# A four-layer graph network on one core: 23 single source blocks instead of 15, the maximum as one reduction, and a node stage spread over three engines

## The chip, the cores and the metric

The kernel runs on one core of one Trainium2 chip. The metric is the device time of one launch in microseconds (us). A launch holds everything: sorting out the graph, encoding nodes and edges, four layers, and the output. Lower is better.

## The reference

There are 6250 nodes with 64 features and 206,250 directed edges (100,000 pairs in both directions and one self loop per node), sorted by target node. `h` is the encoded node table, `e` the encoded edge table. Four layers of this run one after the other:

```
msg   = relu(h[src] + e) + 1e-7                # one row of 64 per edge
m     = msg * t                                # t: one number per layer
ex    = exp(m - segment_max(m, dst)[dst])      # softmax over a node's edges
agg   = segment_sum(msg * ex, dst) / segment_sum(ex, dst)
z     = relu(layernorm((h + agg) @ w1 + b1) * g1 + bb1)
h_new = z @ w2 + b2                            # added to h from the second layer on
```

Between layers `h` goes through a layer normalization, gain, bias and relu; behind the last one the input `x` is added.

## The kernel before

**Stage 1** (`prepare`) encodes edges and nodes and works out which edges belong to which node. **Stage 2** (`lay`) puts the 6250 nodes into 49 blocks of 128 (one node per partition) and gives each block `d` a row of `S[d]` slots of 64 features. The first `G` slots of a block are a grid: slot `s` holds the edge whose source lies in group `s` of source nodes, a group being one source block of 128 or a pair of them. Edges that find no free grid slot go to the `V[d]` overflow slots behind it. Before the change there are 15 single blocks and 17 pairs, so G = 32, and the 49 blocks have 676 overflow slots and 2244 slots in all. For 35 blocks (18 units) stage 2 forms the slot rows with matmuls: for each of the 128 nodes a one-hot matrix `hot` (DVE, L886) times the node's rows in `byk` (PE, L905, five nodes to a PSUM bank, 102 columns each of which 65 are used), copied out by ACT.

**Stage 3** is the four layers (`layer`), three in a loop and one behind it. Within a layer the blocks go by in a fixed order in which large and small rows of slots alternate. For block `d`:

- `gathers(d)`: POOL issues one indirect DMA for each overflow slot, from `ztab` into `gb` (L1228). `gb` has two buffers; the gathers of d+1 wait until `over(d-1)` has read its buffer.
- `load_x(d)`, `load_oh(d)`: SP's queue loads the encoded edges `xb` and the 49 one-hot matrices `oh` of a block (1568 KB), two buffers each. `load_oh(d+2)` waits for the products of block d.
- `passes(d, j)`: PE multiplies `oh` with the node table `zp`, 147 small matmuls (L1243) for a block, for the eight grid slots j of a PSUM bank each; `gps` is a ring of four banks.
- `add(d, j)`: DVE adds a bank of products to `xb` (L1260). `over(d)` adds the gathered rows (L1270).
- `most(d)`: the maximum over the slots, by halving (L1281, five or six operations) and a last one into `top_x` (L1286); ACT makes `cm` of it.
- `sub(d, i)`: per slice of up to 24 slots, relu and minus the maximum (DVE, L1302), then ACT's exp (L1308).
- `mul(d, i)`: relu times the exponential (DVE, L1316), then the slot sums: PE adds the slots with an identity matrix in `both` (L1326), two matmuls of 512 columns for every four slots. `fold(d)` brings them down to 128 columns (L1336).
- `node_unit(u)`: softmax division, linear 1, layer normalization, linear 2, update of `h`, normalization of the next table rows, split into three bf16 parts, scatter to `ztab`; for two blocks at a time. It is a generator that `steps` advances in pieces between the operations above.

All engines run their own instructions in the order in which the code writes them. One trip of the block loop is:

```python
for j in range(JS):
    add(d, j)
    if d + 1 < ND:
        passes(d + 1, j)
    steps(2, "normed")
over(d)
...                      # most(d), sub(d, i), fold(d - 1), node head
for i in range(n):
    mul(d, i)            # and its slot sums on PE
```

So PE's order is: slot sums of block d-1, all 147 products of block d+1, slot sums of block d. The normalization (`norm`) runs on DVE alone; its inverse root is an integer start value and three Newton steps on columns of two numbers (L201 to L220), and the normalized rows are made by L247.

## Time and profile before

| | |
|---|---|
| median of three runs | 6420.68 us (6414.47 to 6424.67) |
| the profiled execution | 6423.57 us, its span 6419.1 us |
| busy: PE, DVE, POOL, ACT | 72%, 75%, 69%, 27% of the span |
| stage 1, 2, 3 | 0 to about 840, to about 1792, to the end |
| a layer of the loop | about 1147 us; the last 1187 us |

A page gives the busy share of each engine over the span; what the time hangs on changes from stage to stage, and within a stage it is seen in the rows in order of time, by what an engine was idle for and until whom.

### The profile page before, as it was taken

The numbers are of one execution on the slowest core, as the hardware profiler recorded it, in microseconds if no ns is written. First come the engines' busy times: TensorE is split into PE (matmuls) and PEld (weight loads), VectorE is DVE, ScalarE is ACT, GpSimd is POOL, SyncE is SP. The second block draws the span as 40 slices with busy tenths as digits, with TensorE's granted clock in tenths as the row PEclk, the third lists the DMA queues.
The fourth block names the chain that finished last, engine by engine and source line by source line (L and its number), as shares of the span: only waits on it lengthen the run. The fifth ranks groups of instructions, "written<-read, shape, count | busy, mean of one in ns | idle before, by whom it ended". The sixth has DMA issues, their size and how long they took to land. (4 is left out here: it accounts for less than half of the span.)

```text
span 6419.1 us, 112465 instructions
## 1 busy us (share of the span) xinstructions
PE 4606.3 (72%) x44676; PEld 3217.7 (50%) x44676; DVE 4837.2 (75%) x10914; ACT 1753.4 (27%) x2619; POOL 4403.1 (69%) x3850
## 2 busy tenths in 40 slices
PE   6716888899947777773777777377777746767776
PEld 6705778888834444442444444244444433444443
DVE  9432555544359999994999999499999958888887
ACT  2403778666611111110111111011111101111111
POOL 2054767666357777875777777477777747777776
PEclk8956988776668888886888888688888878888887
DMA  8962565544365555544555554445555534444442
GB/s 346 417 205 81 211 224 197 214 179 164 124 202 164 168 178 171 169 130 128 169 170 174 166 170 159 115 156 176 170 171 171 168 124 141 162 158 165 158 158 85
DMA packets 313907, 1116.65 MB, mean 174 GB/s; under 512 B 138994, under 2 KB 142244, under 8 KB 252308
## 3 DMA queue, kind: packets, MB, share of 16 engines
q1 hardware_dynamic: 163444, 839.13, 35.3%
q0 software_dynamic: 134800, 214.63, 13.7%
q10 hardware_dynamic: 15120, 55.50, 2.1%
q8 instruction: 360, 5.90, 0.4%
q14 instruction: 183, 1.50, 0.1%
HBM read 859.44 MB, written 249.52 MB: 173 GB/s over the span
## 5 line engine op out<-in xcount | busy, mean ns | idle before, releaser
L1228 POOL DMA_INDIRECT gb<-ztab,ovi x2704 | 3158.9, 1168 | 971.2 <-issue 825.2
L1326 PE MATMUL bank<-ep_mid,keep 128*128 128x512 f32 (+3 forms) x3474 | 1610.3, 623 | 18.0 <-DVE ep_mid L1316 18.0
L1326 PEld LDWEIGHTS bank<-ep_mid,keep 128*128 128x128 f32 x3474 | 709.6, 207 | 884.3 <-issue 819.5
L1379 PE MATMUL bank<-keep,na 128*128 128x128 f32 x100 | 47.5, 475 | 1028.6 <-DVE na L1376 1028.6
L1292 ACT ACTIVATE cm<-top_x,nt 128x64 f32<-128x64 f32 x196 | 68.2, 348 | 2569.7 <-DVE top_x L1286 2569.7
L1065 POOL DMA_INDIRECT ecell<-zpw,ptg x588 | 611.2, 1040 | 226.9 <-issue 177.1
L1243 PE MATMUL bank<-zpw,oh_mid 128*128 128x64 bf16 x21609 | 660.4, 194 | 108.8 <-DMA oh_mid<-ohd 102.9
L1243 PEld LDWEIGHTS bank<-zpw,oh_mid 128*128 128x128 bf16 x21609 | 656.2, 98 | 150.2 <-issue 139.6
L905 PE MATMUL bank<-byk,zpw 88*88 88x102 f32 (+13 forms) x4608 | 639.3, 314 | 17.1 <-DVE zpw L886 13.2
L905 PEld LDWEIGHTS bank<-byk,zpw 88*88 88x88 f32 (+13 forms) x4608 | 607.9, 216 | 22.9 <-DVE zpw L886 15.7
L1260 DVE TENSOR_TENSOR xb<-bank,xb 128x512 f32<-128x512 f32 x784 | 535.6, 686 | 90.5 <-DMA xb<-ecell 90.2
L1326 PE MATMUL bank<-ep_last,keep 128*128 128x512 f32 (+3 forms) x1158 | 550.4, 636 | 2.9 <-DVE ep_last L1316 2.9
L1379 PEld LDWEIGHTS bank<-keep,na 128*128 128x128 f32 x100 | 18.2, 182 | 1040.8 <-DVE na L1376 1040.8
L886 DVE TENSOR_TENSOR zpw<-keep,kct 88x440 f32<-88x440 f32 (+13 forms) x468 | 291.8, 634 | 288.4 <-PE bank L905 284.2
L1308 ACT ACTIVATE ep_mid<-ep_mid,pack 128x1280 f32<-128x1280 f32 (+10 forms) x327 | 444.8, 1390 | 218.0 <-DVE ep_mid L1302 214.8
L1302 DVE SCALAR_TENSOR_TENSOR ep_mid<-xb,top_x 128x1280 f32<-128x1280 f32 (+10 forms) x327 | 489.2, 1540 | 14.9
L1316 DVE SCALAR_TENSOR_TENSOR ep_mid<-xb,ep_mid 128x1280 f32<-128x1280 f32 (+10 forms) x327 | 489.0, 1523 | 0.5 <-ACT ep_mid L1308 0.5
L1281 DVE TENSOR_TENSOR mx<-mx 128x128 f32<-128x128 f32 (+10 forms) x788 | 429.5, 545 | 20.0
L1270 DVE TENSOR_TENSOR xb<-gb,xb 128x768 f32<-128x768 f32 (+17 forms) x196 | 211.7, 1080 | 276.1 <-DMA gb<-ztab,ovi 275.3
L1326 PEld LDWEIGHTS bank<-ep_last,keep 128*128 128x128 f32 x1158 | 241.7, 212 | 300.2 <-issue 281.2
L1457 POOL DMA_INDIRECT ztab<-zb,wri x147 | 203.3, 1383 | 214.3 <-DVE zb L1448 172.5
L1281 DVE TENSOR_TENSOR mx<-xb 128x1408 f32<-128x1408 f32 (+10 forms) x196 | 332.7, 1697 | 3.1
(222 smaller groups left out, 6604.6 us busy)
## 6 DMA issues: line engine op xcount, KB each, us to landing
oh_mid<-ohd SPq DMA_DIRECT2D x147, 1568.0 KB
oh_last<-ohd SPq DMA_DIRECT2D x49, 1568.0 KB
ea_in<-in_ea SPq DMA_DIRECT2D x101, 512.0 KB, 8.2
enc<-es_out ACTq DMA_DIRECT2D x101, 512.0 KB, 8.8
gb<-ztab,ovi POOLq DMA_INDIRECT x2704
ohd<-oh_lay SPq DMA_DIRECT2D x49, 576.0 KB
xb<-ecell SPq DMA_DIRECT2D x20, 1408.0 KB
ohd<-oh_lay SPq DMA_DIRECT2D x49, 512.0 KB
```

What stands on the lines that cost most here:

```text
L886: k["hot"][g] = V(VE.tensor_tensor(hot[0:kp, g % 3, 0:n, 0:mp], iota1[0:kp, None, 0:mp].broadcast_to([kp, n, mp]), kct[0:kp, a:a + n][:, : ...
L905: q = PE.matmul(b[0:mp, WIDE * j:WIDE * j + WIDE], hot[0:kp, g % 3, j, 0:mp], byk[0:kp, at_d:at_d + WIDE], start=True, stop=True)
L1065: at["sc"][j, h] = sc_l[h](GP.indirect_dma_start(T["ecell"], bass.IndirectOffsetOnAxis(ap=ptg[:, j % 2, e:e + 1], axis=0), prows[:, h, a:a ...
L1228: at["g"][d] = ga_l[d % 2](GP.indirect_dma_start(gb[d % 2][:, 64 * v:64 * v + 64], None, T["ztab"], bass.IndirectOffsetOnAxis(ap=ovi[:, i: ...
L1243: q = PE.matmul(gps[j % n_gp][:, 64 * (s % 8):64 * (s % 8) + 64], oh[:, d % 2, at_oh:at_oh + 128], zp[:, b, 64 * part:64 * part + 64], sta ...
L1260: k["add"][d] = V(VE.tensor_tensor(x, gps[j % n_gp][:, 0:64 * (hi - lo)], x, ALU.add))
L1270: k["over"][d] = V(VE.tensor_tensor(x, gb[d % 2][:, 0:64 * S.V[d]], x, ALU.add))
L1281: q = V(VE.tensor_tensor(mx[:, 0:64 * m], src[:, 0:64 * m], src[:, 64 * (n - m):64 * n], ALU.max))
L1302: k["sub"][d, i] = V(VE.scalar_tensor_tensor(ep[:, r, 0:b - a, 64:128], x_of(d, a, b).rearrange("p (s f) -> p s f", f=64), 0.0, top_x[:, d ...
L1308: k["exp"][d, i] = A(AE.activation(ep[:, r, 0:b - a, 0:64], ep[:, r, 0:b - a, 64:128], ACT.Exp, scale=tcol))
L1316: k["mul"][d, i] = k["mul"][d] = V(VE.scalar_tensor_tensor(ep[:, r, 0:b - a, 64:128], x_of(d, a, b).rearrange("p (s f) -> p s f", f=64), 0 ...
L1326: q = PE.matmul(both[d % 2][:, 0:w], ident, rows[:, 128 * (c - a):128 * (c - a) + w], start=(c == 0), stop=(c + 4 >= S.S[d]), skip_group_c ...
```

## The change

It has these parts:

1. 23 single source blocks and 13 pairs: G = 36 grid slots, 634 overflow slots and 2398 slots in all; the largest row has 72 slots. A block's products are still 147 matmuls, but fill five banks' worth (the fifth 4 slots wide), JS = 5 over the ring of four.
2. `add` and `passes` go through the ring by one running count `JS * d + j`. `load_x(d+1)` now stands ahead of `load_oh(d+2)`.
3. The maximum is one `tensor_reduce` over a view of `xb` in which the slots run innermost (64 columns apart), and one `tensor_scalar`.
4. `norm` takes its inverse root from ACT (Ln, then Exp), polishes it with one Newton step on DVE, and lets ACT write the normalized rows. The biases b1 and b2 come in by a matmul with the identity, `cm` times `npd` and the three bf16 parts move to ACT. A part named "gap" ends a round of `steps` early where DVE would wait for ACT.
5. In stage 2 seven nodes to a bank, 65 columns a product, `hot` with two buffers of seven nodes instead of three of five.

```diff
-        self.singles = 15
+        self.singles = 23
@@ norm
-            q = V(VE.tensor_scalar(nwf[:, 0, :], mv[:, :, 1], LN_EPS, None, ALU.add))
+            root, half, by, shift = (nwf[:, i, :] for i in range(4))
+            q = V(VE.tensor_scalar(half, mv[:, :, 1], LN_EPS, -0.5, ALU.add, ALU.mult))
+
+            AE.wait_ge(ve_s, q)
+            q = A(AE.activation(by, half, ACT.Ln, scale=-2.0))
+            AE.wait_ge(ae_s, q)
+            q = A(AE.activation(root, by, ACT.Exp, scale=-0.5))
+            yield "gap"
+            VE.wait_ge(ae_s, q)
...
             for s in (0, 1):
-                q = V(VE.tensor_scalar(out[:, s, 0:width], src[:, s, 0:width], mv[:, s, 0:1],
-                                       nwf[:, 1, s:s + 1], ALU.subtract, ALU.mult))
+                q = A(AE.activation(out[:, s, 0:width], src[:, s, 0:width], ACT.Identity,
+                                    bias=shift[:, s:s + 1], scale=root[:, s:s + 1]))
@@ spread (stage 2)
-                            q = PE.matmul(b[0:mp, WIDE * j:WIDE * j + WIDE],
-                                          hot[0:kp, g % 3, j, 0:mp],
-                                          byk[0:kp, at_d:at_d + WIDE], start=True, stop=True)
+                            q = PE.matmul(b[0:mp, 65 * j:65 * j + 65], hot[0:kp, g % 2, j, 0:mp],
+                                          byk[0:kp, at_d:at_d + 65], start=True, stop=True)
@@ add
-                    nxt = (d, j + n_gp) if j + n_gp < JS else (d + 1, j % n_gp)
-                    before_pass[nxt] = k["add"][d]
+                    before_pass[divmod(c + n_gp, JS)] = k["add"][d]
@@ most
-                    while n > 2:
-                        m = -(-n // 2)
-                        vwait(q)
-                        q = V(VE.tensor_tensor(mx[:, 0:64 * m], src[:, 0:64 * m],
-                                               src[:, 64 * (n - m):64 * n], ALU.max))
+                    q = V(VE.tensor_reduce(mx[:, 0:64], x_of(d, 0, S.S[d]).rearrange(
+                        "p (s f) -> p f s", f=64), AX.X, ALU.max))
@@ node_unit
-                    for i, d in enumerate(blocks):
-                        VE.wait_ge(ae_s, k["cm"][d])
-                        q = V(VE.tensor_scalar(cm[:, u % 2, i, :], cm[:, u % 2, i, :],
-                                               npd[:, d:d + 1], None, ALU.mult))
...
-                    V(VE.tensor_tensor(h[:, u, :], h[:, u, :], b2, ALU.add))
...
+                    PE.matmul(NA[:, 0:256], ident, b1, start=True, stop=False)
...
-                        q = V(VE.tensor_copy(to, left))
+                        q = A(AE.copy(to, left))
@@ block loop
-                for j in range(JS):
+                for j in range(n_gp):
                     passes(0, j)
                 for d in range(ND):
                     if d + 1 < ND:
                         gathers(d + 1)
-                        if d + 2 < ND:
-                            load_oh(d + 2)
                         load_x(d + 1)
...
                     for j in range(JS):
                         add(d, j)
-                        if d + 1 < ND:
-                            passes(d + 1, j)
+                        to = divmod(JS * d + j + n_gp, JS)
+                        if to[0] < ND:
+                            passes(*to)
+                        if j == JS - n_gp - 1 and d + 2 < ND:
+                            load_oh(d + 2)
                         steps(2, "normed")
```

Where instructions stand on the engines, at three places. First PE in a layer of the loop, from the slot sums of a large block to the next slot sums. A row ends in the semaphores that its first instruction waits for; m1 is DVE's counter, m2 ACT's, m13 and m14 the loads of `oh`. Before:

```order
L1326 MATMUL bank<-ep_mid,keep 128x512 [waits m1]
L1326 MATMUL bank<-ep_mid,keep 128x512 x4
L1326 MATMUL bank<-ep_mid,keep 128x384
L1243 MATMUL bank<-zpw,oh_mid 128x64 [waits m1,m14]
L1243 MATMUL bank<-zpw,oh_mid 128x64 x23
L1243 MATMUL bank<-zpw,oh_mid 128x64 [waits m1]
L1243 MATMUL bank<-zpw,oh_mid 128x64 x26
L1243 MATMUL bank<-zpw,oh_mid 128x64 [waits m1]
L1243 MATMUL bank<-zpw,oh_mid 128x64 x47
L1243 MATMUL bank<-zpw,oh_mid 128x64 [waits m1]
L1243 MATMUL bank<-zpw,oh_mid 128x64 x47
L1396 MATMUL bank<-keep,hb 128x128 [waits m1]
```

And with the change:

```order
L1330 MATMUL bank<-ep_mid,keep 128x512 [waits m1]
L1330 MATMUL bank<-ep_mid,keep 128x512
L1330 MATMUL bank<-ep_mid,keep 128x256
L1249 MATMUL bank<-zpw,oh_mid 128x64 [waits m1]
L1249 MATMUL bank<-zpw,oh_mid 128x64 x23
L1249 MATMUL bank<-zpw,oh_mid 128x64 [waits m1,m14]
L1249 MATMUL bank<-zpw,oh_mid 128x64 x23
L1249 MATMUL bank<-zpw,oh_mid 128x64 [waits m1]
L1249 MATMUL bank<-zpw,oh_mid 128x64 x23
L1249 MATMUL bank<-zpw,oh_mid 128x64 [waits m1]
L1249 MATMUL bank<-zpw,oh_mid 128x64 x26
L1249 MATMUL bank<-zpw,oh_mid 128x64 [waits m1]
L1249 MATMUL bank<-zpw,oh_mid 128x64 x47
L1392 MATMUL bank<-keep,hb 128x128 [waits m2]
```

Before, the wait for a load of `oh` (m14) stands at the first product behind the sums: all four groups are of the next block. Now a group of 24 products without that wait comes first: the fifth group of the block whose adds are under way.

Second DVE, from the last adds of a block to its differences (m0 is PE's counter; m24, m25, m32 and m33 are those of the gathers and of the `xb` loads). Before, a small block:

```order
L1281 TENSOR_TENSOR mx<-xb 128x1408 [waits m1,m2]
L1281 TENSOR_TENSOR mx<-mx 128x704 [waits m1]
L1281 TENSOR_TENSOR mx<-mx 128x384 [waits m1]
L1281 TENSOR_TENSOR mx<-mx 128x192 [waits m1]
L1281 TENSOR_TENSOR mx<-mx 128x128 [waits m1]
L1286 SCALAR_TENSOR_TENSOR top_x<-mx 128x64 [waits m1]
L1302 SCALAR_TENSOR_TENSOR ep_mid<-xb,top_x 128x24x64 [waits m1,m0]
```

With the change:

```order
L1267 TENSOR_TENSOR xb0<-bank1,xb0 128x512 [waits m0]
L1267 TENSOR_TENSOR xb0<-bank2,xb0 128x256 [waits m0]
L1276 TENSOR_TENSOR xb0<-gb0,xb0 128x448 [waits m32,m24]
L1283 TENSOR_REDUCE mx<-xb0 128x64 [waits m2,m1]
L1287 TENSOR_SCALAR top_x<-mx 128x64 [waits m1]
L1306 SCALAR_TENSOR_TENSOR ep_mid<-xb0,top_x 128x24x64 [waits m1,m0]
```

There is a fifth add of 256 columns, which waits for PE, and two operations stand where six stood.

Third ACT, at the node stage between a small block's exponentials and the next block's `cm`. Before:

```order
L1308 ACTIVATE ep_mid<-ep_mid,pack 128x24x64 [waits m1]
L1308 ACTIVATE ep_mid<-ep_mid,pack 128x19x64 [waits m1]
L1399 ACTIVATE yt<-bank,pack 128x256 [waits m0]
L1440 ACTIVATE z<-na 128x128 [waits m1]
L1292 ACTIVATE cm<-top_x,nt 128x64 [waits m1]
```

With the change:

```order
L1312 ACTIVATE ep_mid<-ep_mid,pack 128x22x64 [waits m1]
L1397 ACTIVATE yt<-bank,pack 128x256 [waits m0]
L245 ACT_TABLE_LOAD
L245 ACTIVATE nwf<-nwf 128x2 [waits m1]
L247 ACT_TABLE_LOAD
L247 ACTIVATE nwf<-nwf 128x2 [waits m2]
L261 ACTIVATE hb<-h,nwf 128x64 [waits m1]
L261 ACTIVATE hb<-h,nwf 128x64
L1440 ACTIVATE z<-na 128x128 [waits m1]
L1448 CAST zb<-zb 128x2x64 [waits m1]
L1448 CAST zb<-zr 128x2x64 [waits m1] x2
L1293 ACTIVATE cm<-top_x,nt 128x64 [waits m1]
```

Ln and Exp each have a table load in front, twice per unit of two blocks.

## Rows read from the trace of the kernel before

**Rows 1.** The page: busy us, share of the span and instructions of each engine.

```profile
PE 4606.3 (72%) x44676; PEld 3217.7 (50%) x44676; DVE 4837.2 (75%) x10914; ACT 1753.4 (27%) x2619; POOL 4403.1 (69%) x3850
```

**Rows 2.** Busy us by stretch: stage 2, a layer of the loop, the last layer.

```profile
core 0: us, PE busy (x) PEld busy (x) DVE busy (x) ACT busy (x) POOL busy (x), PEclk, DMA share, GB/s
840.00:1792.00 952.00, 840.24 (x6372) 789.62 (x6369) 464.36 (x1269) 656.86 (x1127) 572.76 (x556) 0.73 0.49 183
...
2940.00:4088.00 1148.00, 809.16 (x8586) 487.22 (x8586) 986.52 (x2236) 192.34 (x233) 852.07 (x725) 0.84 0.49 159
...
5232.00:6419.00 1187.00, 821.45 (x8586) 492.92 (x8586) 973.49 (x2110) 184.40 (x208) 905.94 (x774) 0.84 0.48 153
```

**Rows 3.** Groups by line, POOL's gathers and DVE's adding of them.

```profile
L1228 POOL DMA_INDIRECT gb<-ztab,ovi x2704 | 3158.9, 1168 | 971.2 <-issue 825.2 <-POOLq L168 91.0 <-DVE xb L1270 18.0
...
L1270 DVE TENSOR_TENSOR xb<-gb,xb 128x768 f32<-128x768 f32 (+17 forms) x196 | 211.7, 1080 | 276.1 <-DMA gb<-ztab,ovi 275.3 <-issue 0.8
```

**Rows 4.** ACT in time: first and last of a layer's 49 `cm`, two layers.

```profile
2971.62 0.35 ACT L1292 ACTIVATE cm<-top_x,nt 128x64 f32<-128x64 f32 x1 [46.82 <-DVE top_x L1286]
...
4032.06 0.35 ACT L1292 ACTIVATE cm<-top_x,nt 128x64 f32<-128x64 f32 x1 [13.34 <-DVE top_x L1286]
...
5264.56 0.35 ACT L1292 ACTIVATE cm<-top_x,nt 128x64 f32<-128x64 f32 x1 [46.08 <-DVE top_x L1286]
...
6376.76 0.35 ACT L1292 ACTIVATE cm<-top_x,nt 128x64 f32<-128x64 f32 x1 [15.48 <-DVE top_x L1286]
```

**Rows 5.** PE and DVE in time, from a large block's sums on (start, us).

```profile
2699.81 3.29 DVE L1316 SCALAR_TENSOR_TENSOR ep_mid<-xb,ep_mid 128x1536 f32<-128x1536 f32 x2
2701.79 11.41 PE L1326 MATMUL bank<-ep_mid,keep 128*128 128x512 f32 x24
2707.43 0.69 DVE L1260 TENSOR_TENSOR xb<-bank,xb 128x512 f32<-128x512 f32 x1
2713.04 4.45 PE L1243 MATMUL bank<-zpw,oh_mid 128*128 128x64 bf16 x147
2717.26 0.68 DVE L1336 TENSOR_REDUCE ds<-bank 128x128 f32<-128x512 f32 x1
2717.86 1.74 DVE L1316 SCALAR_TENSOR_TENSOR ep_mid<-xb,ep_mid 128x1536 f32<-128x1536 f32 x1
2719.79 9.66 PE L1326 MATMUL bank<-ep_mid,keep 128*128 128x512 f32 x22
2726.86 0.68 DVE L1260 TENSOR_TENSOR xb<-bank,xb 128x512 f32<-128x512 f32 x1
2740.08 0.42 DVE L1355 TENSOR_SCALAR cm<-cm,npd 128x64 f32<-128x64 f32 x2
2742.86 3.29 DVE L1316 SCALAR_TENSOR_TENSOR ep_mid<-xb,ep_mid 128x1536 f32<-128x1536 f32 x2
```

**Rows 6.** Groups by line with shapes apart: the reductions there are.

```profile
L634 DVE TENSOR_REDUCE nod<-floats 128x49 f32<-128x3136 f32 x1 | 5.7, 5709 | 0.0
L504 DVE TENSOR_REDUCE ext<-same 128x1 f32<-128x1728 f32 x1 | 2.0, 1953 | 0.0
```

**Rows 7.** Groups by line: DVE's differences and maxima.

```profile
L1302 DVE SCALAR_TENSOR_TENSOR ep_mid<-xb,top_x 128x1280 f32<-128x1280 f32 (+10 forms) x327 | 489.2, 1540 | 14.9
...
L1302 DVE SCALAR_TENSOR_TENSOR ep_last<-xb,top_x 128x1280 f32<-128x1280 f32 (+11 forms) x109 | 163.9, 1547 | 5.0
...
L1281 DVE TENSOR_TENSOR mx<-mx 128x128 f32<-128x128 f32 (+10 forms) x788 | 429.5, 545 | 20.0
L1281 DVE TENSOR_TENSOR mx<-xb 128x1408 f32<-128x1408 f32 (+10 forms) x196 | 332.7, 1697 | 3.1
```

**Rows 8.** Groups by line: the table load, the root's steps, stage 2's products and broadcasts.

```profile
L396 ACT ACT_TABLE_LOAD x1 | 1.3, 1283 | 3.0 <-issue 3.0
...
L905 PE MATMUL bank<-byk,zpw 88*88 88x102 f32 (+13 forms) x4608 | 639.3, 314 | 17.1 <-DVE zpw L886 13.2 <-ACT byk L824 3.0 <-ACT edge L824 0.6
L968 PE MATMUL bank<-idb,lct 128*128 128x128 bf16 x1568 | 176.4, 251 | 24.4 <-DVE lct L955 23.0 <-DVE ovi L956 0.7 <-ACT cb L977 0.2
```

More of the change, by code:

```diff
@@ L229, in straight, with norm @@
                     return e.value
-        def norm(V, src, width, out):
+        def norm(V, A, src, width, out):
             for s in (0, 1):
@@ L240, in norm @@
             vwait(q)
-            q = V(VE.tensor_scalar(nwf[:, 0, :], mv[:, :, 1], LN_EPS, None, ALU.add))
+            root, half, by, shift = (nwf[:, i, :] for i in range(4))
[6 more added lines that the diff above has]
+            VE.wait_ge(ae_s, q)
+            for c in (0, 1):
+                q = V(VE.scalar_tensor_tensor(by[:, c:c + 1], root[:, c:c + 1], half[:, c:c + 1],
+                                              root[:, c:c + 1], ALU.mult, ALU.mult))
             yield
-            q = yield from rsqrt_steps(V, nwf[:, 0, :], nwf[:, 1, :], nwf[:, 2, :],
-                                       nwf[:, 3, :], nwi[:, 0, :], q)
             vwait(q)
+            q = V(VE.scalar_tensor_tensor(root, by, 1.5, root, ALU.add, ALU.mult))
+            yield
+            vwait(q)
+            q = V(VE.scalar_tensor_tensor(shift, mv[:, :, 0], -1.0, root, ALU.mult, ALU.mult))
+            AE.wait_ge(ve_s, q)
             for s in (0, 1):
-                q = V(VE.tensor_scalar(out[:, s, 0:width], src[:, s, 0:width], mv[:, s, 0:1],
-                                       nwf[:, 1, s:s + 1], ALU.subtract, ALU.mult))
-            yield
+                q = A(AE.activation(out[:, s, 0:width], src[:, s, 0:width], ACT.Identity,
+                                    bias=shift[:, s:s + 1], scale=root[:, s:s + 1]))
             return q
@@ L876, in spread @@
                 VE.wait_ge(ae_s, k["kct"][u])
-                starts = list(range(0, 128, 5))
+                starts = list(range(0, 128, 7))
                 first = n_hot[0]
@@ L1125, in lay @@
                 pass
-            steps = 26 + 1 + 16 + 64 // 5
+            steps = 19 + 1 + 16 + 64 // 5
             making, share = iter(()), 0.0
@@ L1291, in most @@
                         AE.wait_ge(ve_s, k["node", "den"][u - 2])
-                    k["cm"][d] = A(AE.activation(cm[:, u % 2, i, :], top_x[:, d % 2, :], ACT.Exp,
-                                                 scale=nt[:, 0:1]))
+                    q = A(AE.activation(cm[:, u % 2, i, :], top_x[:, d % 2, :], ACT.Exp,
+                                        scale=nt[:, 0:1]))
+                    AE.wait_ge(ae_s, q)
+                    k["cm"][d] = A(AE.activation(cm[:, u % 2, i, :], cm[:, u % 2, i, :],
+                                                 ACT.Identity, scale=npd[:, d:d + 1]))
                 def sub(d, i):
@@ L1409, in node_unit @@
                     vwait(q)
-                    q = yield from norm(V, h[:, u, :].rearrange("p (s f) -> p s f", s=2), 64, hb)
-                    vwait(q)
+                    q = yield from norm(V, A, h[:, u, :].rearrange("p (s f) -> p s f", s=2), 64,
+                                        hb)
+                    yield "gap"
+                    VE.wait_ge(ae_s, q)
                     q = V(VE.tensor_tensor(na[:, 1, :, :], hb[:, :, 0:64],
@@ L1467, in steps @@
                             part = next(now["unit"], "end")
+                            if part == "gap":
+                                if n < 99:
+                                    return
+                                continue
                             now["part"] = part or now["part"]
@@ L1715, in node_pair @@
                 vwait(k_hb)
-                q = yield from norm(V, hb, 128, hb)
-                PE.wait_ge(ve_s, q)
+                q = yield from norm(V, A, hb, 128, hb)
+                PE.wait_ge(ae_s, q)
                 for s in (0, 1):
```

88 lines of the change are left out of this document (40 added, 48 removed).

## The prediction, made before the run

> **What bounds the kernel now.** The page first: PE, DVE and POOL are each busy 69 to 75% of the span [rows 1], which names no bound. So by stretch: stage 2 takes 952 us with PE busy for 840, at a granted clock of 0.73; a layer of the loop takes 1148, with DVE busy for 987, POOL for 852 and PE for 809 [rows 2]. Then the groups: POOL's 2704 gathers take 1.168 us each and were preceded by 825.2 us of mere issue, (3158.9 + 825.2) / 2704 = 1.47 us a gather; it waited for DVE for 18 us in all, while DVE waited 275.3 us for gathers [rows 3]. So in the layers POOL issues without a break and DVE, nearly full, is just behind it. The blocks' pace is in ACT's `cm`, one a block: from the first to the 49th a layer of the loop needs 4032.06 - 2971.62 = 1060 us, the last one 6376.76 - 5264.56 = 1112 [rows 4]. That is 42 to 46 us for a pair of a large and a small block.
>
> In order of time [rows 5] the reader is to see who does not wait: the large block's multiplications begin at 2699.81; PE sums its slots from 2701.79 to 2713.2, and DVE meanwhile goes through the adds of the next block, the fourth of which ends at 2708.12. DVE needs no result of PE's until the `fold` at 2717.26. PE lags by 5 us and nobody pays.
>
> **The change, part by part.**
>
> *The fifth group of products.* PE now has the order: slot sums of d-1, fifth group of d, products of d+1. The fourth add can be as early as it likes; the fifth waits for PE to finish the sums that it was allowed to lag with. From there DVE's work on d stands in a row (fifth add, over, maximum, differences, fold), and only its first multiplication lets PE begin the next sums. The stage turns into a chain in which PE and DVE take turns. What lies in PE's shadow costs nothing: later multiplications, normalization steps, four adds. I sum the chain over a layer (49 blocks, 2398 slots, 634 overflow slots, 617 groups of four):
>
> - Slot sums, 2 x 617 = 1234 matmuls. 22 took 9.66 us, 0.439 each; 24 took 11.41, 0.9 more than that rate gives [rows 5]. I take 542 for them and 1.2 a block for the slow start behind each idle stretch of PE, there being one before every block now: 600.
> - The fifth group: 24 of the 147 products that take 4.45 us [rows 5] are 0.73, with 0.1 for the handover; 41. Its add has half the columns of the 0.68 us of a full one [rows 5], 0.4 with the fixed part; 20.
> - `over`: 211.7 / 4 = 52.9 [rows 3], times 634/676; 50.
> - Differences: (489.2 + 163.9) / 4 = 163.3 [rows 7], times 2398/2244; 174.
> - The maximum, below; 279. The clamp into `top_x` and its handovers, my estimate from the small steps, 0.25; 12.
> - `fold` 0.68 [rows 5]; 33. The head of a node unit: 2740.08 to 2742.86 less 0.42 for L1355, now on ACT, and 0.2 for b2's add; 2.15 for 24.5 units [rows 5]; 53.
> - Until PE begins its sums: 1.93 from the multiplication's start at 2717.86 to 2719.79, 1.98 at 2699.81 [rows 5], there 0.5 more for the new matmul with b1, and 0.2 for longer exponentials; 2.3, so 113.
>
> The sum is 1375, for 48 intervals of 49 it is 1347, and 10 more for the first pair, which waits for the 36 gathers of its large block: 1357 us against 1060, and 1112 in the last layer, whose extra work on POOL no longer counts. That is 3 x 297 + 245 = 1136.
>
> *The maximum.* By halving it costs (429.5 + 332.7) / 196 = 3.9 us a block [rows 7] and 0.2 for the last step. The reduction reads all slots, 2398 x 64 = 153,472 columns a layer, in steps of 64 columns. Two SBUF reductions are in the trace: adjacent columns, 1728 in 1.953 us, 1.13 ns each; and one that also steps over rows (49 columns apart), 3136 in 5.709 us, 1.82 ns each [rows 6]. I take the second, since its way of reading is that of the new one: 279 us a layer, 5.7 a block, where halving had 4.1. The first is the lower bound (173 a layer); above, I allow 2.3 ns (353). So an operation that reads as fewer instructions costs 1.6 us more a block, and on the chain.
>
> The Trainium skill speaks to this twice. Its page "SBUF — State Buffer", section "SBUF: two separate sides", says that SBUF is read in lines of 16 bytes and that each access to another line pays; the stepping row agrees, no run here separates the cause. Its page "VectorE: DVE Perf Modes", section "The perf-mode tier table", gives a reduction one element a cycle whatever its operands. By that alone the maximum would cost about what the adjacent row says, and the time would be that of rival B.
>
> *The slots.* They grow by 7% and are in the sums above. The 42 gathers fewer a layer are 62 us of POOL at 1.47 [rows 3]; but POOL needs 26 x 1.47 + 4 = 42 us for a pair whose chain takes 56, so their worth is nothing here. It would be the main gain if the chain did not form.
>
> *The node stage.* DVE loses three Newton steps down to one, the normalized rows, two biases and the casts, some 130 us a layer by their groups. All but the head lies in PE's shadow and is given back as waiting. The way through ACT costs two table loads of 1.283 us [rows 8] and two small activations, 3.3 us per normalization, against covers of one add (0.68) and one multiplication (1.5): DVE stands still for 2.6 + 1.8 us per unit. In the large block's shadow DVE is then at its fourth add about 11 us after the multiplications began, where the sums end at 15. So this too is hidden. Without that cover it is 4.4 x 24.5 = 108 us a layer. At the end of a layer nothing covers it: two units, four normalizations, 2 us each, 8 us a layer, 32 in all.
>
> A price that only a page has: the Trainium skill, page "ScalarE: Activation LUTs", section "What ACT_TABLE_LOAD costs", puts a switch at 2.66 us with its drain. By it a normalization waits for 5.9 us and DVE reaches the fourth add at 14, still inside; the sum would stay.
>
> *Loads.* `load_oh(d+2)` is issued later, behind the fifth group of d, and is needed one block (28 us) on, behind the sums of d+1. At the 159 GB/s of the stage [rows 2] its 1.6 MB take 10 us. Hidden.
>
> *Stage 2.* The products take 639.3 us [rows 8], weight load and columns one behind the other: (65 + 88) of (102 + 88) columns, 0.81, is 120 us less at an equal clock. Against it stand 196 more broadcasts at 0.11 (176.4 / 1568) [rows 8], 22 us, DVE with one buffer less to run ahead in, and PE's clock, which was at 0.73 with 102 columns and may be granted less with 65; were all products at 1.2 GHz, the gain would be gone. Between -110 and +60 I take -40.
>
> **Sum.** The profiled execution took 6423.6 us (3 over the median). 6423.6 + 1136 + 32 - 40 = 7552; I say 7550.
>
> **The rivals.**
>
> - **B: the chain forms, the maximum reads at the adjacent rate.** 106 us a layer less: 7550 - 424 = 7130. For it speaks L504's row, against it L634's, a single instruction. 0.20.
> - **C: the chain does not form and gathers set the pace: faster.** Decided by one point: whether PE has ended the sums and the fifth group before DVE is through with four adds. Then a layer follows POOL, 62 us less: 6424 - 4 x 62 - 40 = 6135. Against it: the sums end 13.4 us after the multiplications began, the adds 8.3 [rows 5]; sums would have to shrink to 60%, or ACT's waits grow by 4 us a block. 0.08.
> - **D: no chain, but DVE gives back on ACT what it saved.** 130 us less and 108 more, slots and fifth add 45 more, the maximum 0 to 77 more: within 0.2% to somewhat slower, 6430 to 6700. It hangs on C's point. 0.04, half of it within 0.2%.
> - **E: the chain and more.** The maximum at 2.3 ns, 296 more, or ACT's waits outside the shadow, or a lower clock on the sums, which now stand in the chain: at 1.2 GHz throughout they would double. About 7900. 0.08.
> - The forecast itself (A below) has 0.60.
>
> 0.2% is about what a measurement of this kernel can tell from no change. Slower is A, B, E and half of D, 0.90; within 0.2%, 0.02; faster, 0.08. The range 7000 to 7800 holds A and B with the bounds of the unknown costs, leaving out C, D and most of E; A alone has 7400 to 7700.
>
> **What the profile afterwards would show.** DVE's idle time goes to the fifth add and is ended by PE's products, some 4 us a large-to-small turn. POOL waits for DVE's `over` instead of issuing without a break. `cm` comes every 28 us, 56 for a pair. The reduction takes 5 to 6 us; at 3.3 it is B. ACT holds 401 table loads, 515 us busy, with DVE waiting on ACT before L251. The busy share of all three engines falls in the layers, PE's to near 0.65. Stage 2's products go from 0.139 us each to near 0.11 if the clock holds. Wrong would be the whole argument if the fifth add waited for nobody; wrong in size, most likely the reduction, or the slow start of the sums.

## The result, and the profile after

The changed kernel takes 7666.36 us (median of 4, 7664.81 to 7676.54) where the kernel before takes 6417.58 (median of 4). The ratio is 1.195, 95% interval 1.1933 to 1.1968. The profiled execution took 7676.5 us, 1252.9 more than that of before.

The page's first part, to be held against [rows 1]:

```profile
PE 5141.7 (67%) x45575; PEld 3662.9 (48%) x45576; DVE 4901.6 (64%) x7685; ACT 2692.3 (35%) x4220; POOL 3959.3 (52%) x3682
```

No engine but ACT is busier in share than before: most of the added time is waiting. The view by stretch (columns as in [rows 2]), first the window that [rows 2] has for stage 2 and then the second layer from its first to its 49th `cm`:

```profile
840.00:1792.00 952.00, 869.41 (x5671) 822.70 (x5670) 420.33 (x1028) 576.68 (x930) 505.87 (x498) 0.62 0.44 165
3459.80:4792.60 1332.80, 857.83 (x8451) 522.81 (x8451) 971.63 (x1376) 411.31 (x636) 719.55 (x656) 0.82 0.41 131
```

The ends of that layer, which answer to [rows 4], in ACT's timeline:

```profile
3459.78 0.35 ACT L1293 ACTIVATE cm<-top_x,nt 128x64 f32<-128x64 f32 x1 [43.10 <-DVE top_x L1287]
...
4792.61 0.35 ACT L1293 ACTIVATE cm<-top_x,nt 128x64 f32<-128x64 f32 x1 [13.19 <-DVE top_x L1287]
```

So the difference can be laid out along the launch. Up to the first `cm`: 1826.36 before, 2041.62 now, +215. The four layers from first to 49th `cm`: 1058.4, 1060.4, 1058.1, 1112.2 before; 1334.5, 1332.8, 1335.9, 1334.0 now, +1048. The three pieces between layers and the end behind the last: 303.5 before, 291.1 now, -12. That is 1251, the whole difference of the spans.

What stands behind the +1048 is in the groups by line (busy us, mean ns of one | idle before them, and until whom):

```profile
L1267 DVE TENSOR_TENSOR xb<-bank,xb 128x512 f32<-128x512 f32 (+1 forms) x980 | 607.0, 633 | 1155.6 <-PE bank L1249 1072.8 <-DMA xb<-ecell 82.8
L1276 DVE TENSOR_TENSOR xb<-gb,xb 128x704 f32<-128x704 f32 (+17 forms) x196 | 198.2, 1011 | 60.3 <-DMA gb<-ztab,ovi 60.3
L1283 DVE TENSOR_REDUCE mx<-xb 128x64 f32<-128x3008 f32 (+17 forms) x196 | 1075.0, 5484 | 6.7
L251 DVE SCALAR_TENSOR_TENSOR nwf<-nwf 128x1 f32<-128x1 f32 x400 | 70.7, 219 | 160.3 <-ACT nwf L247 158.8
L1234 POOL DMA_INDIRECT gb<-ztab,ovi x2536 | 2792.5, 1101 | 1933.9 <-DVE xb L1276 1085.9 <-issue 745.9 <-POOLq L168 90.8
L1330 PE MATMUL bank<-ep_mid,keep 128*128 128x512 f32 (+2 forms) x3702 | 1768.8, 639 | 22.9 <-DVE ep_mid L1320 22.9
```

DVE stands still for 1072.8 us at its adds until PE's products are there (nothing before), and POOL for 1085.9 until DVE's `over`; in [rows 3] that was 18. In order of time all of the 1072.8 us lie before the fifth add of a block, at 192 of 196 blocks, 5.6 us each in the mean; the other four adds never waited for PE. The forecast had some 4 us at one of the two turns of a pair; it is about 4 to 5 at the one and 6 at the other. One turn of it in PE's and DVE's timeline, the counterpart of [rows 5]:

```profile
4192.58 3.29 DVE L1306 SCALAR_TENSOR_TENSOR ep_mid<-xb,top_x 128x1536 f32<-128x1536 f32 x2
4195.79 0.69 DVE L1340 TENSOR_REDUCE ds<-bank 128x128 f32<-128x512 f32 x1
4196.39 1.75 DVE L1320 SCALAR_TENSOR_TENSOR ep_mid<-xb,ep_mid 128x1536 f32<-128x1536 f32 x1
4198.79 11.83 PE L1330 MATMUL bank<-ep_mid,keep 128*128 128x512 f32 x24
4201.99 0.35 DVE L251 SCALAR_TENSOR_TENSOR nwf<-nwf 128x1 f32<-128x1 f32 x2 [0.26 <-ACT nwf L247]
4205.70 0.69 DVE L1267 TENSOR_TENSOR xb<-bank,xb 128x512 f32<-128x512 f32 x1
4210.46 4.45 PE L1249 MATMUL bank<-zpw,oh_mid 128*128 128x64 bf16 x147
4211.36 0.42 DVE L1267 TENSOR_TENSOR xb<-bank,xb 128x256 f32<-128x256 f32 x1 [4.77 <-PE bank L1249]
4212.88 5.70 DVE L1283 TENSOR_REDUCE mx<-xb 128x64 f32<-128x3264 f32 x1
4218.61 0.20 DVE L1287 TENSOR_SCALAR top_x<-mx 128x64 f32<-128x64 f32 x1
```

PE's sums cannot start before DVE's multiplication at 4196.39; DVE's fourth add is over at 4206.4, the sums run to 4210.46, and only behind them does PE come to the fifth group (the first 24 of the 147 products, which the view shows as one piece with those of the next block), for which the fifth add has waited 4.77 us. Then everything of the block stands in a row on DVE. The engines take turns.

### The profile page after: what moved, and what is told of

It reads as the page before. It is cut to its first block and busy times, and to the rows that moved or that the text cites. A ratio compares the mean times of both kernels' runs of the same rounds, so it can differ in the third digit from the quotient of the medians.

```text
span 7669.9 us, 112339 instructions
## 1 busy us (share of the span) xinstructions
PE 5141.7 (67%) x45575; PEld 3662.9 (48%) x45576; DVE 4901.6 (64%) x7685; ACT 2692.3 (35%) x4220; POOL 3959.3 (52%) x3682
## 5 line engine op out<-in xcount | busy, mean ns | idle before, releaser
L1234 POOL DMA_INDIRECT gb<-ztab,ovi x2536 | 2792.5, 1101 | 1933.9 <-DVE xb L1276 1085.9
L1330 PE MATMUL bank<-ep_mid,keep 128*128 128x512 f32 (+2 forms) x3702 | 1768.8, 639 | 22.9 <-DVE ep_mid L1320 22.9
L1267 DVE TENSOR_TENSOR xb<-bank,xb 128x512 f32<-128x512 f32 (+1 forms) x980 | 607.0, 633 | 1155.6 <-PE bank L1249 1072.8
L1283 DVE TENSOR_REDUCE mx<-xb 128x64 f32<-128x3008 f32 (+17 forms) x196 | 1075.0, 5484 | 6.7
L913 PE MATMUL bank<-byk,zpw 88*94 88x65 f32 (+13 forms) x4608 | 810.7, 372 | 14.3 <-DVE zpw L896 10.4
L913 PEld LDWEIGHTS bank<-byk,zpw 88*94 88x94 f32 (+13 forms) x4608 | 791.4, 288 | 21.2 <-DVE zpw L896 14.5
L896 DVE TENSOR_TENSOR zpw<-keep,kct 88x658 f32<-88x658 f32 (+16 forms) x342 | 289.3, 850 | 447.9 <-PE bank L913 446.5
L1312 ACT ACTIVATE ep_mid<-ep_mid,pack 128x1280 f32<-128x1280 f32 (+13 forms) x363 | 479.6, 1348 | 153.8 <-DVE ep_mid L1306 149.0
L1306 DVE SCALAR_TENSOR_TENSOR ep_mid<-xb,top_x 128x1280 f32<-128x1280 f32 (+13 forms) x363 | 518.2, 1477 | 14.9
L1320 DVE SCALAR_TENSOR_TENSOR ep_mid<-xb,ep_mid 128x1280 f32<-128x1280 f32 (+13 forms) x363 | 522.6, 1472 | 1.3 <-ACT ep_mid L1312 1.3
```

Of the source, the lines that this page charges most:

```text
L896: k["hot"][g] = V(VE.tensor_tensor(hot[0:kp, g % 2, 0:n, 0:mp], iota1[0:kp, None, 0:mp].broadcast_to([kp, n, mp]), kct[0:kp, a:a + n][:, : ...
L913: q = PE.matmul(b[0:mp, 65 * j:65 * j + 65], hot[0:kp, g % 2, j, 0:mp], byk[0:kp, at_d:at_d + 65], start=True, stop=True)
L1234: at["g"][d] = ga_l[d % 2](GP.indirect_dma_start(gb[d % 2][:, 64 * v:64 * v + 64], None, T["ztab"], bass.IndirectOffsetOnAxis(ap=ovi[:, i: ...
L1267: k["add"][d] = V(VE.tensor_tensor(x, gps[c % n_gp][:, 0:64 * (hi - lo)], x, ALU.add))
L1283: q = V(VE.tensor_reduce(mx[:, 0:64], x_of(d, 0, S.S[d]).rearrange("p (s f) -> p f s", f=64), AX.X, ALU.max))
L1306: k["sub"][d, i] = V(VE.scalar_tensor_tensor(ep[:, r, 0:b - a, 64:128], x_of(d, a, b).rearrange("p (s f) -> p s f", f=64), 0.0, top_x[:, d ...
```

## The experiments

All twelve ran on three chips on which the kernel before itself took 8150 to 8620 us; a ratio below is to the kernel before on the same chip, and "the first chip" is that of the result above. What is different there can be seen in PE's timeline of the kernel before with the new stage 2, `e5_before65` (the lines are of a layer, which is that of before):

```profile
4323.52 0.31 PE L1237 MATMUL bank<-zpw,oh_mid 128*128 128x64 bf16 x5 [0.45 <-issue]
4324.26 0.31 PE L1237 MATMUL bank<-zpw,oh_mid 128*128 128x64 bf16 x5 [0.43 <-issue]
4325.02 0.28 PE L1237 MATMUL bank<-zpw,oh_mid 128*128 128x64 bf16 x4 [0.45 <-issue]
```

The same 147 products that took 4.45 us in one piece [rows 5] come in heaps of five with pauses that nothing in the profile ends. I read them as PE waiting for its own instructions; no run tries that reading, and why it happens on these chips is open. Where PE idles anyway, the pauses cost little (with the stage 2 of before the changed kernel's layers are 1343 to 1348 us on one of the chips and 1374 to 1379 on another, 1334 on the first); where PE had been free to run, they become a bound of their own. So layers and stretches are compared, by their `cm`, rather than totals.

**Stage 2 as before: `e1_wide`, and with 65 columns: `e2_five65`.** Both are the changed kernel with five nodes to a bank and three buffers; `e1_wide` has 102 columns a product too, `e2_five65` keeps 65. The edit of the first, in part:

```diff
-                            q = PE.matmul(b[0:mp, 65 * j:65 * j + 65], hot[0:kp, g % 2, j, 0:mp],
-                                          byk[0:kp, at_d:at_d + 65], start=True, stop=True)
+                            q = PE.matmul(b[0:mp, WIDE * j:WIDE * j + WIDE], hot[0:kp, g % 3, j, 0:mp],
+                                          byk[0:kp, at_d:at_d + WIDE], start=True, stop=True)
```

> The changed kernel with stage 2's products as before the change: 102 columns, five nodes to a bank, three buffers. Theory 1 (the products lost PE's full clock and that is what stage 2 lost): L913's 4608 matmuls go back from 0.176 to near 0.139 us each, the granted clock of the stage from 0.62 to above 0.7, and the time from 7666 to about 7475 (7440 to 7510). Rival 1 (stage 2 is longer because of the 36 grid slots: more broadcasts, wider rows): the time stays within 25 us of 7666.

> The changed kernel with five nodes to a bank and three buffers, but 65 columns a product. Theory 1 (the number of columns decides the clock): as the changed kernel, 7640 to 7690, the clock of stage 2 at 0.60 to 0.64. Rival 2 (seven nodes to a bank with one buffer less is what costs): about 7475, as with all of stage 2's products undone.

Measured: 8459.2 and 8453.0 us, ratios 1.0359 (1.0314 to 1.0405) and 1.0357 (1.0314 to 1.0401). The first `cm` came at 2690 and 2703. The totals do not differ, and the times that were expected are out of reach on such a chip; but the width alone moves the granted clock. The view by stretch, 526 to 1826, first with 102 and then with 65 columns:

```profile
526.00:1826.00 1300.00, 821.84 (x5467) 735.26 (x5466) 407.90 (x1039) 573.04 (x959) 479.23 (x483) 0.65 0.30 113
```

```profile
526.00:1826.00 1300.00, 861.45 (x5300) 793.79 (x5299) 390.97 (x1001) 562.98 (x938) 469.88 (x475) 0.58 0.28 108
```

With 65 columns PE is busy longer for fewer instructions, at 0.58 instead of 0.65. By the trace's clock records 1165 of the 4608 products ran at the full clock with 102 columns, and 93 with 65.

**The other way round: `e5_before65`, the kernel before with the new stage 2 (seven nodes, two buffers, 65 columns), and `e1b_wide` beside it.**

> The kernel before with stage 2 alone changed: seven nodes to a bank, 65 columns, two buffers of hot. If this change is what costs the 215 us up to the first cm: the first cm moves from 1826 to about 2040 and the whole is 6420 + 215, a ratio of about 1.033, with the products' granted clock at 0.62. If the 215 us come from the larger grid (more rows in stage 2) or from the code ahead of it: first cm within 30 us of 1826, ratio 1.000 to 1.005. Layers as before in both, 1060 and 1112.

> The changed kernel with before's stage 2 (102 columns, five nodes to a bank, three buffers), the same kernel as in the first set of runs. Counterpart to the kernel before with the new stage 2: if the narrow products cost the time, first cm comes at about 1830 to 1860 and the whole is about 7475, a ratio of 1.165; if they don't, it stays near 7666, a ratio of 1.195. Layers 1334 in both cases.

Measured: 8621.0 us, ratio 1.0008 (0.9978 to 1.0039), and 8625.7, ratio 1.0026 (1.0002 to 1.005). The first `cm` came at 2658 and 2721. By the letter the ratio of `e5_before65` is the one expected if the new stage 2 costs nothing. But I can judge neither expectation by it: the pauses ahead of the products of stage 2 come to 250 us in the one and 301 in the other, none on the first chip, and may cover what the clock costs. The clock did fall: 104 of the 4608 products of `e5_before65` ran at the full clock, 1299 of those of `e1b_wide`.

Seven nodes to a bank with two buffers did no harm on these chips. `e3_tree` and `e4_fifth`, below, have the whole new stage 2 on the chip of `e2_five65` and reach their first `cm` at 2623 and 2602, where five nodes and three buffers at the same width came to 2703. Nor did the larger grid cost much: on the chip of `e5_before65`, `e4b_fifth` with 36 grid slots has its first `cm` at 2666 and `e7_grid32` with 32 at 2641; on the third chip `e4c_fifth` has it at 2613 and `e7c_grid32` at 2634. Runs with one and the same stage 2 on the first of these chips spread from 2589 to 2632.

**The maximum by halving: `e3_tree`.** The changed kernel with before's `most`; the edit in part:

```diff
-                    q = V(VE.tensor_reduce(mx[:, 0:64], x_of(d, 0, S.S[d]).rearrange(
-                        "p (s f) -> p f s", f=64), AX.X, ALU.max))
+                    while n > 2:
+                        m = -(-n // 2)
+                        vwait(q)
+                        q = V(VE.tensor_tensor(mx[:, 0:64 * m], src[:, 0:64 * m],
+                                               src[:, 64 * (n - m):64 * n], ALU.max))
```

> The changed kernel with the maximum by halving as before. Theory 2 (the maximum stands in the chain between PE's fifth group and PE's next sums, so its whole difference shows): the reduction's 5.48 us against 4.16 for halving at the new slots, 1.3 less for each of 196 blocks, 7666 - 255 = 7410 (7390 to 7470, as small node steps may come in between its levels). Rival 3 (it lies in a shadow, the sums' pace decides alone): 7640 to 7680.

Measured: 8220.6 us, ratio 1.0079 (1.0054 to 1.0104). Loop layers of 1296 us against 1345 with the reduction on the same chip (`e1_wide`, whose layers are those of the change), 49 less; against `e2_five65` it is 46, and 35 in the last layer. Its groups:

```profile
L1287 DVE TENSOR_TENSOR mx<-mx 128x128 f32<-128x128 f32 (+9 forms) x788 | 448.2, 569 | 27.2
L1287 DVE TENSOR_TENSOR mx<-xb 128x1536 f32<-128x1536 f32 (+9 forms) x196 | 354.0, 1806 | 19.8
...
L1335 PE MATMUL bank<-ep_mid,keep 128*128 128x512 f32 (+2 forms) x3702 | 1852.7, 664 | 17.8 <-DVE ep_mid L1325 17.8
```

Halving is (1073.0 - 802.2) / 4 = 68 us a layer shorter than the reduction was in `e1_wide`, and 49 of them arrive, so the maximum does stand in the chain, and the one instruction is the slower way to take it. The sums grew: the group has 1777.6 us in `e1_wide` and 1852.7 here over three layers, 25 us a layer, which is about what is missing. It is the clock that made them longer. Averaged over the sums alone, the granted clock is 0.884 in `e1_wide` and 0.848 here, and clock times busy time is 1571.5 us in both.

**A fifth bank in the ring: `e4_fifth`, `e4b_fifth`, `e4c_fifth`.** Bank 7 joins the ring, and what it held moves to the upper half of bank 6. Now all 147 products of d+1 again stand behind the sums of d-1, none of block d. The loads of `oh` are issued where they were before the change, and b1's matmul stands behind a wait; the edit in part:

```diff
-                n_gp = 4
+                n_gp = 5
-                gps = bank[0:4]
-                both, NA, NB = bank[4:6], bank[6], bank[7]
+                gps = bank[0:4] + bank[7:8]
+                both, NA, NB = bank[4:6], bank[6], bank[6][:, 256:512]
```

> The changed kernel with five banks for the products (the node stage's two half banks share one), so that all products of d+1 are issued behind the adds of d and none of d stands behind the slot sums of d-1. Theory 3 (the fifth group made a chain of PE and DVE): the idle time before the adds, 1073 us until PE's products, falls under 100, a layer's 49 blocks take about 1160 us instead of 1334, bound by DVE with its waits for ACT, and the time is about 6970 (6850 to 7100). Rival 4 (the blocks' pace is set by the waits for ACT or by the reduction, and the fifth group only shows where DVE happens to wait): above 7500.

> The changed kernel with a fifth bank in the ring (bank 7, whose use moves into the upper half of bank 6), the same kernel as in the first set of runs. Theory: the fifth group no longer waits behind the slot sums, so the chain opens; DVE then carries a layer with its own work (slots up 7%, reduction 5.5 us a block): 1150 to 1220 us a layer against 1334, a ratio to before of 1.06 to 1.12. Rival (as the first set of runs hints, where it was slower than the changed kernel): all 147 products stand as one heap ahead of linear 1 and of the slot sums, and the node stage's results come late instead; then layers are 1300 or more and DVE's wait stands at L1405 and at the first st of the fold's unit.

> The same kernel as e4_fifth and e4b_fifth (the changed kernel with five banks in the ring), for the same reason. Theory: layers of 1150 to 1220 against 1334, DVE's wait before its adds gone, ratio 1.06 to 1.12. Rival: all 147 products as one heap ahead of linear 1 delay the node stage, DVE waits at the first statistics of a unit and before L1405 instead, and layers stay at 1300 or more.

Measured: 8585.6, 8842.7 and 8584.8 us, ratios 1.0533, 1.0276 and 1.0533; loop layers of 1372 to 1382, 1430 to 1447 and 1374 to 1384, longer than with the chain on two of these chips (1345 and 1377; none was run on the third). My expectation of the size failed three times, and what was written down as the rival of the second and third is what came: layers over 1300, with DVE waiting at the first statistics and before L1405. The groups of the third:

```profile
L1267 DVE TENSOR_TENSOR xb<-bank,xb 128x512 f32<-128x512 f32 (+1 forms) x980 | 595.0, 630 | 235.8 <-remote 174.9 <-issue 46.0 <-PE bank L1249 7.8
L234 DVE BATCH_NORM_STATS2 st<-bank 128x6 f32<-128x128 f32 x200 | 49.5, 289 | 809.7 <-PE bank L1384 799.5 <-issue 10.2
L1405 DVE TENSOR_TENSOR h<-h,bank 128x128 f32<-128x128 f32 x100 | 28.8, 288 | 629.2 <-PE bank L1401 629.2
...
L1249 PE MATMUL bank<-zpw,oh_mid 128*128 128x64 bf16 x21609 | 1105.0, 210 | 991.9 <-issue 889.1 <-DMA oh_mid<-ohd 96.5 <-DVE na L1361 1.0
```

The 1073 us of waiting at the adds are gone, as the chain theory says (7.8 are left). But 889 us of pauses now stand ahead of PE's products, linear 1 and 2 stand behind them, and DVE waits for those. On these chips one bound may have hidden the other, or the products in one heap may be in the way by themselves: these runs cannot tell.

**The grid of before: `e7_grid32`, `e7c_grid32`.** The changed kernel with 15 single blocks, G = 32 and four groups to a block; the loads of `oh` are issued where they were before the change, all else of it is kept.

> The changed kernel with the grid of before (15 single blocks, G = 32, four groups of products to a block over the ring of four banks), all else of the change kept: maximum as one reduction, normalization on ACT, stage 2 with 65 columns. Theory (the fifth group, which must wait behind the slot sums, makes the chain of PE and DVE): no add waits behind the sums any more, a layer goes from about 1334 us (first to 49th cm) back to between 1060 and 1120, DVE's idle time before its adds falls from over 1000 us to under 100, and what stays over the kernel before is stage 2's 215 us plus 0 to 200 in the layers: 6400 to 6850 where before takes 6420, a ratio of 1.03 to 1.07. Rival (the reduction, the way through ACT or a lower clock makes the layers long, not the fifth group): layers stay over 1250 us.

> The same kernel as e7_grid32 (the changed kernel with the grid of before), once more, in the hope of a chip on which the kernel before takes its 6420 us; where it took 8157 and 8616, PE stood still in its products for want of instructions, which hides what is asked here. Theory (the fifth group makes the chain): layers of 1060 to 1120 us from first to 49th cm against 1334, under 100 us of idle time before DVE's adds, a ratio to before of 1.03 to 1.07 (stage 2's 215 us and 0 to 200 in the layers). Rival (reduction, ACT or clock make the layers long): layers over 1250, ratio over 1.14. If PE's products come again in small heaps with pauses ended by nothing, the run decides only the part of the wait that DVE shows.

Measured: 8692.4 and 8430.7 us, ratios 1.0101 (1.0054 to 1.0148) and 1.0348 (1.0328 to 1.0369); loop layers of 1390 to 1406 and 1338 to 1343, where 1060 to 1120 had been expected and over 1250 was the rival's sign. The wait at the adds for PE fell to 74.9 and 64.6 us, but the pauses ahead of the products came to 1011 and 957 us in the loop. The same picture, and the size as open as before.

**A third of the products: `e9_after49` and `e10_five49`.** These two make the chips' own bound smaller. Only the first of the three bf16 parts of `zp` is multiplied, so the two lower parts are left out of the grid rows; 49 products to a block, and the first kernel keeps every wait of the changed one. The second has the fifth bank too, with the same moves beside it as in `e4_fifth`.

```diff
-                            for part in range(3):
+                            for part in range(1):
```

> The changed kernel with one of the three bf16 parts of the node table multiplied instead of all three: 49 products to a block and not 147 (the two lower parts are left out of the grid rows). On the chips of the other experiments PE stood still in its products for want of instructions; with a third of them it should not. All waits stay, the fifth group's (8 products now) too. It is the control for e10_five49. Theory (chain through the fifth group): a layer from first to 49th cm is the changed kernel's 1334 less 49 times 0.5 us for the 16 products fewer in the chain, 1310; DVE's wait at its adds for PE's products stays about 1000 us or more. Rival (the sums would be early if the 147 products were not in their way, or supply of instructions made the length): 1100 to 1200.

> The same 49 products to a block, and a fifth bank in the ring (bank 7, whose use moves to the upper half of bank 6), so that the fifth group no longer stands behind the slot sums. Theory: nothing but DVE's own work (951 us busy in a layer of the changed kernel) and POOL's 634 gathers (932 us at 1.47) is left, with some 40 us a layer of waits for ACT: 1040 to 1180 us from first to 49th cm, 130 to 270 less than e9_after49; the wait at the adds for PE's products is gone. Rival 1 (reduction, clock or normalization make the layers long, not the fifth group): within 60 us of e9_after49. Rival 2 (the waits move): layers fall by less than 130, and DVE's idle time reappears at the first statistics of a unit or at L1405, ended by PE.

Measured: 8264.1 us, ratio 1.013 (1.01 to 1.0159), and 7673.7, ratio 0.9406 (0.9333 to 0.9479), which is no gain over before, since two thirds of the products are gone. Loop layers: 1328.0, 1328.2, 1317.5 against 1161.5, 1157.5, 1156.2, **166 us a layer for the fifth bank**; the last layer 1338.1 against 1216.5, 122. From one layer's first `cm` to the next layer's, with the piece between them, it is 152 to 168. For the loop layers this is what the chain theory expected (about 1310; 1040 to 1180, 130 to 270 less), and not within 60 us as the first rival had it. Of the second rival a part came: DVE's wait before L1405 is 314 us, 100 in the changed kernel. The view by stretch of each one's second layer, first `cm` to 49th, without and with the bank:

```profile
4019.30:5347.50 1328.20, 749.49 (x3837) 397.94 (x3836) 966.56 (x1376) 411.35 (x637) 710.31 (x642) 0.76 0.40 131
```

```profile
3909.90:5067.40 1157.50, 774.12 (x3819) 411.17 (x3820) 969.18 (x1376) 414.46 (x636) 707.42 (x634) 0.79 0.46 151
```

Busy times are nearly the same (PE's 25 us more with the bank); only the waiting left. The add's group without the bank, and then with it:

```profile
L1267 DVE TENSOR_TENSOR xb<-bank,xb 128x512 f32<-128x512 f32 (+1 forms) x980 | 607.2, 632 | 1281.0 <-PE bank L1249 1079.7 <-remote 107.2 <-DMA xb<-ecell 85.5
```

```profile
L1267 DVE TENSOR_TENSOR xb<-bank,xb 128x512 f32<-128x512 f32 (+1 forms) x980 | 594.7, 629 | 208.8 <-remote 124.9 <-DMA xb<-ecell 66.3 <-issue 17.5
```

The wait for PE is gone from it (`remote` is idle time ended by an event that the profile gives to no instruction), and the wait for loads of `xb`, which the moved load of `oh` could have changed, differs by 19 us in the whole launch. DVE in `e10_five49`, the fourth and fifth add of a block in its timeline:

```profile
4993.84 0.68 DVE L1267 TENSOR_TENSOR xb<-bank,xb 128x512 f32<-128x512 f32 x1
...
4994.64 0.41 DVE L1267 TENSOR_TENSOR xb<-bank,xb 128x256 f32<-128x256 f32 x1
4994.97 1.01 DVE L1276 TENSOR_TENSOR xb<-gb,xb 128x832 f32<-128x832 f32 x1
```

The pauses are not gone here either. PE's products in the loop:

```profile
L1249 PE MATMUL bank<-zpw,oh_mid 128*128 128x64 bf16 x7203 | 336.0, 199 | 520.9 <-issue 443.1 <-DMA oh_mid<-ohd 72.1 <-DVE ep_mid L1306 3.6
```

Late in that layer, where few pauses are left (1.0 to 1.6 us a pair), the last nine pairs took 43.4 to 44.7 us, 44.2 in the mean, against 54.2 to 54.8 with the chain. Before the change a pair took 41.0 to 46.1 (the first of a layer left out), 43.0 in the mean. So even without the chain the larger grid, with the reduction, would by these pairs have brought nothing in the layers. DVE is then the fullest engine, busy for 360 of the last 397 us of that layer, where before POOL set the pace with DVE just behind.

## Why the prediction came true, and where it did not

7550 us were forecast, with 7400 to 7700 for the likeliest case; it was 7666. The mechanism of the layers is A: the pair `e9_after49` and `e10_five49` shows the chain, on another chip and with a third of the products, and the waits of the changed kernel's own trace agree with it. The total is in part luck. Three errors hide in it, of opposite signs: the layers came to 88 us less than forecast, the pieces between and behind them to 44 less, and stage 2 to 255 more. That is 123 in sum, from 7552 to the 7675 of the profiled execution.

- **The chain.** Forecast 1357 us for a loop layer, measured 1334; forecast +1136 for all four, measured +1048. Its terms, forecast in brackets: the sums 1768.8 / 3 = 590 a layer (600); the handover to the fifth add 0.90 (0.83); `over` 198.2 / 4 = 50 (50); PE's start 2.40 behind the multiplication in the turn above and 2.11 in the other (2.3). The sums and the maximum were each about 10 too large, which is most of the 23. By the clock records the sums would take 524 a layer at the full clock; all above that is the granted clock, 0.888 over the sums now and 0.915 before.
- **The maximum.** 1075.0 / 4 = 269 us a layer against 279, 1.75 ns a column. The stepping row of [rows 6] was the right one, and B fell by it. The Trainium skill's page "VectorE: DVE Perf Modes", section "The perf-mode tier table", gives a reduction one element a cycle whatever its operands; the adjacent row may be read so, this one not, and the measurement decides.
- **The normalization.** DVE waited 158.8 us at L251 in 200 normalizations, 0.8 each, and was through with four adds 10 us after the multiplications began, the sums after 14; 11 and 15 were forecast. Hidden, as said. Uncovered, in `e10_five49`, the same wait came to 153.6, some 38 a layer where I had priced 108: D's price was too high. D's range was added up wrongly besides: its own terms (130 less, 108 and 45 more, the maximum 0 to 77 more, stage 2 with 40 less) give 6476 to 6784, not 6430 to 6700.
- **Gathers.** 1085.9 us of POOL's waiting for DVE show that their saving was worth nothing. And C falls twice: the chain formed, and where it was opened, POOL waited for DVE for 102 us in the launch instead of 1086, and a pair still took longer than before.
- **The ends of the layers.** +32 forecast, -12 measured. I charged ACT's way there and not the Newton steps and rows that DVE no longer does in the same place. That this is the reason is argued, not tried.
- **Stage 2: the step that failed.** "Between -110 and +60 I take -40": it was +215. First, I put its start at 840; its first product is at 546.50 before the change and at 547.96 with it. From 526 to the first `cm` PE is busy for 1124 us of 1300 before and for 1349 of 1515 now: 225 more busy time in a stretch 215 longer, so PE's own work is what the stage gained. Second, the price of a product went by columns and weights with the clock left alone as a risk. PE's timeline of the kernel before, in products of two units:

```profile
646.56 2.71 PE L905 MATMUL bank<-byk,zpw 108*110 108x102 f32 x26
...
1139.57 3.66 PE L905 MATMUL bank<-byk,zpw 92*94 92x102 f32 x20
```

and of the changed one, in the same two units:

```profile
643.61 5.62 PE L913 MATMUL bank<-byk,zpw 108*116 108x65 f32 x28
...
1457.48 4.87 PE L913 MATMUL bank<-byk,zpw 92*98 92x65 f32 x28
```

What clock was granted in these stretches, by the view by stretch (us, PE busy, PEclk, DMA share, GB/s), of before:

```profile
646.50:649.20 2.70, 2.70 (x32) 1.00 0.81 314
...
1139.00:1144.00 5.00, 5.00 (x34) 0.50 0.48 120
```

and of the changed kernel:

```profile
643.60:649.00 5.40, 5.40 (x30) 0.50 0.05 18
...
1457.00:1463.00 6.00, 6.00 (x41) 0.50 0.96 365
```

The first wide row gives 0.104 us a product, at 2.4 GHz, the second 0.183, at 1.2 GHz; the narrow ones give 0.201 and 0.174, both at 1.2 GHz. So in the second unit, the one with rows at the same clock, the narrower product saves 5% (with weights 4 columns wider), not the 19% that I took. From start to start over the whole stage, at 1.2 GHz, it is 186 ns for a wide and 182 for a narrow one. And half of the wide products had the full clock: by the trace's clock records 2388 of the 4608 before, and not one now. The view of the products by line:

```profile
L913 PE MATMUL bank<-byk,zpw 88*94 88x65 f32 (+13 forms) x4608 | 810.7, 372 | 14.3 <-DVE zpw L896 10.4 <-ACT byk L834 3.0 <-ACT edge L834 0.5
L974 PE MATMUL bank<-idb,lct 128*128 128x128 bf16 x1764 | 219.7, 275 | 22.2 <-DVE lct L961 7.7 <-ACT cb L983 7.0 <-DVE oh_lay L997 5.6
```

They are 171 us more than in [rows 8], the broadcasts 43, 214 of the 225 together. My +60 stood for "all products at 1.2 GHz" and supposed that their gain would then just be gone; in fact they cost 171 us more, since half of them lost the full clock that their price of 0.139 us had in it. `e1_wide` against `e2_five65` shows that width alone lowers the clock; how much of the 215 us it is on the first chip was not measured.

Open is whether the changed kernel with five banks beats 6420 us on a chip without the pauses. From the pairs of `e10_five49`, 43.4 to 44.7 us even with a third of the products, and the 215 us of stage 2, I would say not.

## What to carry to other kernels

Look for which results an engine is allowed to deliver late. A ring one buffer too short for a block puts one group behind work that was late by design, and the slack of both engines is gone; the busy shares show none of it, the idle time before the consumer's last piece shows all of it. When a matmul is made narrower, ask what clock it will be granted and price it from a row at that clock. Add up an estimate by stretches of the launch, and compare it so: a total can be right by errors that cancel.

## What the runs showed of the hardware

- Products of 65 columns were granted 1.2 GHz where those of 102 had 2.4 GHz in part: none against 2388 of 4608 on the first chip (clock of the window 840 to 1792 0.62 and 0.73), and 93 against 1165 with width alone changed (0.58 and 0.65 from 526 to 1826).
- The duration of the slot sums follows the clock alone. Granted clock over the sums times their busy time is 1571 to 1572 us in every run with 3702 of them in the loop, on all chips, with clocks from 0.848 to 0.926.
- With two thirds of the products left out, PE's clock fell and the sums in the chain grew: on one chip 641 ns a matmul with a layer's clock at 0.80 in `e1_wide`, 661 at 0.76 in `e9_after49`. By the group's busy time that is 21 us a layer, nearly what the 16 products fewer in the chain were to bring (24). Against 1334 on the first chip `e9_after49` had loop layers 6 to 17 us shorter and a last one 4 us longer.
- On three chips PE's small products came in heaps of five per 0.75 us, and the kernel before took 8150 to 8620 us there instead of 6420. In `e5_before65` an add took the same 686 ns as on the first chip, a gather 1115 instead of 1168 and a sum's matmul 660 instead of 623. The changed kernel, whose PE waits anyway, lost 9 to 45 us a layer.
- A maximum that steps 64 columns between elements took 1.75 ns a column, the adjacent reduction 1.13.
